# Attention and feed-forward in one kernel: the turned features leave PSUM on VectorE in two of eight slots

## What is computed

```python
q = layernorm(x)                                   # per token, over 256 features
u = einsum('hbqd,hbkd->hbqk', heads(q), heads(ctx)) * scale / sqrt(16)
attn = softmax(where(mask, -inf, tanh(u) * exp(log_C)))
x = x + merge(einsum('hbqk,hbkd->hbqd', attn, heads(ctx))) @ W_out.T

f = layernorm(x)                                   # "the features"
gf = global_net(f.mean(axis=1))                    # one number per batch
out = f
for _ in range(3):
    tf = sigmoid(gelu(gelu(gelu(out @ w1 + b1) @ w2 + b2) @ w3 + b3) @ w4 + b4)
    coupling = 0.1 + adaptive_range * (0.7 * gf + 0.3 * tf - 0.5) * 2
    out = out + coupling * twist(out)              # twist permutes and negates quarters
x = x + out
```

## Time and profile before

| | us |
|---|---|
| median of 3 runs | 1073.47 (1073.15 to 1073.99) |
| the profiled execution | 1072.12 |
| its span, first to last instruction | 1070.2 |
| TensorE, matmuls: busy | 977.3 |
| ScalarE: busy | 901.5 |
| VectorE: busy | 843.8 |
| GpSimd: busy | 573.9 |
| `features`, its 128 copies on ScalarE: busy | 48.7 |
| `features`, its 128 reads of the accumulator: busy | 28.8 |

### The profile page before, as it was taken

How to read it: one execution, slowest core, us unless ns; L and a number is a source line. 1 busy time by engine, 2 the same in 40 slices (tenths; PEclk the granted TensorE clock), 3 DMA queues, 4 the chain that set the end, 5 groups by cost and what they waited for, 6 DMA issues and landing times.

```text
span 1070.2 us, 21910 instructions
## 1 busy us (share of the span) xinstructions
PE 977.3 (91%) x7260; PEld 526.2 (49%) x7260; DVE 843.8 (79%) x1770; ACT 901.5 (84%) x1121; POOL 573.9 (54%) x1053
## 2 busy tenths in 40 slices
PE   6899999999899999999999999999989999996993
PEld 4456435554355544555445543555435554454431
DVE  3888796997879886987869879699796988688485
ACT  3999778997799978998789977899779997895575
POOL 3366604876068740887228870487606874087204
PEclk7999999999999999999999999999999999999897
DMA  5433002430033200432005310153002430020002
GB/s 118 88 59 58 6 2 44 103 88 1 1 75 89 71 1 1 98 89 48 1 1 118 88 30 1 36 112 88 0 2 69 92 74 1 2 54 31 11 1 80
DMA packets 191119, 51.71 MB, mean 48 GB/s; under 512 B 165920, under 2 KB 174624, under 8 KB 191008
## 3 DMA queue, kind: packets, MB, share of 16 engines
q1 hardware_dynamic: 191008, 50.31, 22.2%
HBM read 33.37 MB, written 16.78 MB: 47 GB/s over the span
## 4 chain that ended last, share of the span: by engine, by line
PE 43%; DVE 16%; POOL 14%; ACT 13%; issue 10%; SPq 2%; DMA 1%; DVEq 0%; POOLq 0%; ACTq 0%
PE ps L1255 8%; PE ps L1269 7%; PE ps L1239 6%; PE ps L1159 5%; ACT probs L914 5%; PE ps L1190 4%; ACT probs L920 3%; PE ps L1175 3%; POOL f_hat L470 3%; PE ps L1278 2%; POOL twisted L525 2%; DVE move_u L780 2%; DVE move_u L801 2%; DVE move_v L782 2%; POOL q_hat L449 2%
## 5 line engine op out<-in xcount | busy, mean ns | idle before, releaser
L914 ACT ACTIVATE probs<-ps,u_scale 120x2048 f32<-120x2048 f32 x128 | 253.7, 1982 | 23.2 <-PE ps L1159 23.2
L920 ACT ACTIVATE probs<-probs,exp_bias,clip 120x2048 f32<-120x2048 f32 x128 | 270.2, 2111 | 0.1
L1269 PE MATMUL ps<-h,w 128*128 128x512 f32 x384 | 185.5, 605 | 14.5 <-ACT h L948 13.8
L1159 PE MATMUL ps<-q_t,k_t 32*120 32x256 f32 x2048 | 148.9, 405 | 21.5 <-ACT probs L914 20.6
L489 POOL TENSOR_TENSOR c<-tok_c 128x16 f32<-128x16 f32 x8 | 1.8, 223 | 277.8 <-issue 277.8
L1190 PE MATMUL ps<-wo_t,of_t 128*128 128x256 f32 x512 | 143.5, 403 | 1.0 <-DVE xy L717 1.0
L692 DVE STREAM_TRANSPOSE o_t<-ps 128x512 f32<-128x512 f32 x128 | 90.6, 708 | 68.0 <-PE ps L1175 67.7
L1175 PE MATMUL ps<-probs,va 120*32 120x256 f32 x2048 | 138.7, 389 | 1.6 <-ACT probs L920 1.5
L1159 PEld LDWEIGHTS ps<-q_t,k_t 32*120 32x120 f32 x2048 | 93.4, 180 | 58.7 <-issue 51.4
L1269 PEld LDWEIGHTS ps<-h,w 128*128 128x128 f32 x384 | 67.5, 189 | 93.0 <-issue 66.0
L1190 PEld LDWEIGHTS ps<-wo_t,of_t 128*128 128x128 f32 x512 | 86.9, 189 | 49.9 <-issue 41.7
(11 more groups left out here) (132 smaller groups left out, 1791.5 us busy)
## 6 DMA issues: line engine op xcount, KB each, us to landing
xy<-in_x_dram SPq DMA_DIRECT2D x64, 256.0 KB, 3.3
out_dram<-xy SPq DMA_DIRECT2D x64, 256.0 KB, 2.1
cbuf<-in_ctx_dram SPq DMA_DIRECT2D x64, 120.0 KB, 2.8
va<-in_ctx_dram SPq DMA_DIRECT2D x64, 120.0 KB, 3.6
tok_c<-coup SPq DMA_DIRECT2D x256, 0.5 KB, 2.0
move_v<-in_L_xattn_W_out_dram SPq DMA_DIRECT2D x1, 256.0 KB, 5.2
move_u<-in_L_ffn_cn_w_dram SPq DMA_DIRECT2D x1, 256.0 KB, 3.3
w<-in_L_ffn_cn_w_dram SPq DMA_DIRECT2D x1, 128.0 KB, 3.1
```

What stands on the lines that cost most here:

```text
L914: eng.activation(probs[:, b % 2, n * HALF:(n + 1) * HALF, :].rearrange("k h q -> k (h q)"), banks(SCORE_BANK, 4)[0:KEYS, :], ACT.Tanh, sca ...
L920: eng.activation(p, p, ACT.Exp, scale=clip[0:KEYS, 0:1], bias=exp_bias[:, b:b + 1]).then_inc(s_exp, 1)
L1159: last = eng.matmul(banks(SCORE_BANK + r)[0:KEYS, odd * S:(odd + 1) * S], k_t[rows, b % 2, odd, n, :], q_t[rows, b % 2, n, :], start=True, ...
L1269: last = eng.matmul(banks(bank), w2[:, k, :], h1[:, p % 2, k, :], start=(k == 0), stop=(k == EK - 1))
```

## The change

In slots of place 1 and 4 (`FEATURES_DVE`), `features(i-3)` is left out on ScalarE, and VectorE does the same work in `features_beside(i-3)`, between `divide` and `attn_features`: two `tensor_scalar` with `accum_out`, with the same waits and the same count on `s_ft`. These are 16 of the 64 batches.

```diff
+        FEATURES_DVE = (1, 4)
...
+            def features_beside(b):
+
+                eng.wait_ge(s_ftr, b + 1)
+                if b >= GROUP:
+                    g, chunk = b // GROUP, b % GROUP // CB
+                    eng.wait_ge(s_h1, EK * (PASSES * (g - 1) + (CYCLES - 1) * CHUNKS + chunk + 1))
+                    eng.wait_ge(s_glob, 3 * g)
+                at = b % GROUP
+                for k in range(EK):
+                    eng.tensor_scalar(f_t[:, k, at * S:(at + 1) * S], banks(TR_BANK)[:, k * S:(k + 1) * S], F_SCALE, None,
+                                      ALU.mult, ALU.add, accum_out=f_sum[:, k, at:at + 1]).then_inc(s_ft, 1)
...
                     if 0 <= here < NB:
                         attn_out(here, 1)
                         divide(here)
+                    if place(i) in FEATURES_DVE and i - LAG < NB:
+                        features_beside(i - LAG)
+                    if 0 <= here < NB:
                         attn_features(here)
...
-                    if 0 <= i - LAG < NB:
+                    if 0 <= i - LAG < NB and place(i) not in FEATURES_DVE:
                         features(i - LAG)
```

## The result

The changed kernel takes 1082.16 us (median of 6, 1080.49 to 1085.37) against 1073.73 us of the kernel before on the same chip (median of 6). The ratio is 1.0086, with a 95% interval of 1.0072 to 1.0100: slower by 0.86%, or 9.2 us; the two medians are 8.4 us apart. The forecast was 1088.7 us with a range of 1079 to 1094.

What follows compares the result with a forecast made beforehand. Bound: the chain VectorE, GpSimd, TensorE, not ScalarE. Groups 1 to 6 12.7 us, group 0 1.5, group 7 1.0, sum 15.2 us on 1072.12 gives 1087.3, plus 1.35 to the median: 1088.7 us, range 1079 to 1094.

Steps and rivals of the forecast that it cites:

- The bound: Attention stage: ScalarE looks full but does not bind; the chain runs VectorE's statistics, GpSimd's steps in order, then TensorE.
- The 0.09 us to TensorE's limit: Slot 20: ScalarE's tanh started at 313.29, TensorE's limit allowed 313.20, so the 0.71 us freed is worth only 0.09 us.
- The price D: VectorE's two added accumulating copies: 2 x (0.41 + 0.12) = 1.06 us a slot, bounds 0.70 and 1.62 us.
- The wait costs nothing: VectorE's added wait for TensorE's turn of the features: turn over at 312.01, VectorE there at about 312.5, so free.
- D counts in full, twice in each of groups 1 to 6: Both changed slots of groups 1 to 6 each lose 1.06 us, nothing gives it back: 12 x 1.06 = 12.7 us.
- GpSimd's order as the link: GpSimd's query scale stands ahead of norm_2, so f_hat hangs on VectorE's new statistics, for which GpSimd waits 0.84 us.
- Group 0 and group 7: Edge groups' losses: 1.5 us in group 0, its two places having nearly the same slack, and 1.0 us in group 7.
- rival B: Half of the added VectorE time is absorbed, by less stretching on GpSimd or one place not counting: 7.6 us, 1081.1 us; 17%.
- Rival A: ScalarE is the bound, so the full 11.4 us come off: 1062.1 us; 5%.
- C: Rival: nothing moves, one side balances the other, within 2 us of 1073.5; 3%.
- E: Rival: GpSimd's order does not bind, so 16 x 0.09 = 1.4 us is gained, 1072.1 us; 3%.
- D by the price: Rival: VectorE's accumulating form is as dear as 512 elements from PSUM, 23.6 us in all, 1097.1 us; 10%.

Runs made afterwards that it cites:

- GpSimd's new order: GpSimd's norm_2 moved ahead of query_scale: on the kernel before 0.9985, 1070.93 us; on the changed kernel 1.0099, 1082.82 us.
- the first experiment: Changed kernel with VectorE's copies cut to one column without the sum, so ScalarE is freed and nothing else: 1.0006 to the kernel before.

## Why the prediction was right, and where its size was off

*The bound.* Right. ScalarE's gapless row was not the bound: freed alone, it gave nothing, where a bound there would have given 11.4 us. The 0.09 us to TensorE's limit was the right reading in kind; the 1.4 us that 16 of them would give did not show either.

*The price D.* This is the term that was mis-sized: 1.06 us against 0.68 us on the queue, just below even the lower bound of 0.70 us, and against 0.57 us of net delay. Two parts: the operation took 0.34 us on the queue, not 0.41, and the accumulator's read took none, not 0.12. The Trainium skill, "VectorE: DVE Perf Modes", § Two Vector instructions with no wait between them, counts an accumulating operation as two instructions, and the trace agrees (32 operations of 0.41 us, 32 reads of 0.08 us), but two instructions are not two times on the queue. The same page of the Trainium skill, § The TRN2 errata, gives an estimated 0.39 us for 256 elements from PSUM, close to the 0.41 us of the row. A third part I had missed: VectorE was not without a gap at that place. Its next start stood 0.74 us behind the division, not 0.63, as it waited for its own result; 0.11 us of D ran there.

*The wait costs nothing.* Right in this kernel: alone it gives 1.0000. The condition that I gave, TensorE 0.5 us later, came true in the kernel with GpSimd's new order, where it held VectorE for 1.17 us.

*D counts in full, twice in each of groups 1 to 6.* Right: 1.20 us in five of the stages, against 2 x 0.57 = 1.14; each place alone costs about half; doubled, the second pair counts in full. With the statistics of the new batch first, the cost in these stages falls from 1.20 to 0.42 us by TensorE, which shows that their lateness is the greater part of what costs in these stages. The rest stays, and by the whole 6 of the 9.2 us do.

*GpSimd's order as the link.* Half right. The chain runs VectorE, GpSimd, TensorE, and GpSimd's wait for the aggregates stays 0.84 us in the changed kernel too, since the steps ahead of it are late by the same: the prediction named it as a sign of being wrong if this wait did not grow towards 1.9 us, and it did not grow. The sign was badly chosen, while the path that it was to show is there. The wait that grew is the one before it in the slot, for the aggregates of `stats_2`: 2.54 us (320.33) against 1.98 (314.91 in the trace of before). And moving f_hat ahead on GpSimd did not take the loss away. The other signs came in the forecast's direction, but smaller: ScalarE's wait 0.47 us for "about 1", TensorE's 0.70 us for f_hat for "about 1" and 1.04 us for q_hat (0.89 before) for 1.9, stages 1.2 us longer for 2.1. ScalarE's busy time fell by 7.0 us and not by 11.4.

*Group 0 and group 7.* 0.96 us against 1.5, 0.59 us against 1.0: in part the same D. But nearly all of group 0's lies in place 1; that its second place has nearly the same slack was wrong.

*The sum.* With 0.57 for 1.06 the same working gives 12 x 0.57 + 2 x (0.57 - 0.27) + (0.57 - 0.1) = 7.9 us, where the attention stages show 9.3. So the price of D made the forecast of 15.2 us too high by 7.3, and 1.4 us the other way, most of it in groups 6 and 0, are not in the working. The result also lies below the 1083.3 us that the prediction's lowest D gives: that it falls inside the range is owed to the room left for rival B, and is luck as far as the size goes. The chances are off by a point: A, C and E have 11% together, "faster" and "within" 12%.

*The rivals.* Rival A is refuted by the first experiment, C and E by the result, D by the price. B's number, 1081.1 us, is closer to the measured 1082.16 than the forecast is, but not for B's reasons: f_hat of slot 21 takes 1.10 us before and after, and both places count. What was half as large was D itself. That a shift of phase changes the stretching is seen, as a loss, in the changed kernel with GpSimd's new order.

## What to carry to other kernels

An engine that is busy without a gap is not the bound if its partner is done 0.1 us before it: compare the two limits at the point where they meet before work is moved off it. Work that is moved to an engine with idle time costs its full time if it lands ahead of what starts a chain through a third engine; here the same two copies cost TensorE 1.20 us in an attention stage, or 0.42 us when the statistics of the new batch stood 1.2 us earlier. Reordering what feeds the chain was worth more than moving work: 0.55% for one moved call. And a stage that is measured between two marks of one engine can change its length because the mark moves; before a gain in one stage and a loss in the next are believed, they are measured again by the engine that bounds them.

## What the runs showed of the hardware

The read of the accumulator on VectorE shows as an instruction of 0.08 us, but the next operation starts at the same time; a copy of 128x256 from PSUM with its sum took 0.34 us on the queue, on ScalarE 0.36 us (312.58 to 312.94 in the earlier trace rows). The two engines are about equal here.

Equal instructions of GpSimd differ in length from slot to slot: the f_hat pair takes 1.10 us in most slots of the kernel before, and 1.57, 1.62 or 2.07 us in the rows above, and moving VectorE's work by half a microsecond changed one from 1.10 to 1.57 us. The Trainium skill, "VectorE: DVE Perf Modes", § Two Vector instructions with no wait between them, names a second SBUF read interface that VectorE shares with GpSimd. No run here isolates it.
